# Moving the product with V from the end of a block to the middle of its score products, in a two-pass attention kernel

## What is computed

```python
x = x + layernorm(attn(layernorm(x)))        # 16 heads of 8 features, 512 x 512 scores per head
x = x + layernorm(ffn(layernorm(x)))         # 128 x 128 products, one sigmoid gate, relu squared
# attn: q = x@Wq+bq ; k = (x@Wk+bk)@Wl+bl ; v = (x@Wv+bv)@Wl+bl
#       softmax(q k^T / sqrt(8)) v, then @ Wo + bo
```

## Time and profile before

| | |
|---|---|
| median of 3 runs | 268.84 us (265.88 to 268.85) |
| the profiled execution | 269.19 us, of which the span of the core 267.3 us |
| share of the span busy | PE 94%, DVE 76%, ACT 67%, PEld and POOL 37% each |
| chain of work that ended last | PE 78%, DVE 13%, ACT 3% |

### The profile page before, as it was taken

How to read it: one execution, slowest core, us unless ns; L and a number is a source line. 1 busy time by engine, 2 the same in 40 slices (tenths; PEclk the granted TensorE clock), 3 DMA queues, 4 the chain that set the end, 5 groups by cost and what they waited for, 6 DMA issues and landing times.

```text
span 267.3 us, 4825 instructions
## 1 busy us (share of the span) xinstructions
PE 250.5 (94%) x1383; PEld 97.6 (37%) x1383; DVE 203.7 (76%) x366; ACT 179.6 (67%) x352; POOL 98.1 (37%) x227
## 2 busy tenths in 40 slices
PE   8996979999999999999999999999999999898981
PEld 4552532232323253234332432343324323332560
DVE  2699688888787888988689889886898998614525
ACT  2573658887787776787677767767677677695132
POOL 6847463010101015551215355512153545214623
PEclk9997799999999999999999999999999999999799
DMA  5346727222030303030304120303031000000101
GB/s 157 99 137 174 213 56 207 60 56 80 13 92 3 88 4 88 2 92 3 88 4 88 41 88 2 88 2 88 2 88 42 2 2 1 4 0 1 39 2 40
DMA packets 13814, 15.65 MB, mean 59 GB/s; under 512 B 3153, under 2 KB 11346, under 8 KB 13794
## 3 DMA queue, kind: packets, MB, share of 16 engines
q1 hardware_dynamic: 13218, 15.15, 20.9%
q10 hardware_dynamic: 576, 0.26, 0.3%
HBM read 11.01 MB, written 4.19 MB: 57 GB/s over the span
## 4 chain that ended last, share of the span: by engine, by line
PE 78%; DVE 13%; ACT 3%; issue 3%; POOL 2%; POOLq 0%; DVEq 0%; ACTq 0%
PE psO L1294 22%; PE psB L1282 20%; PE psA L1263 18%; DVE mx L952 6%; PE psM L1177 3%; PE psM L1183 3%; DVE xh L898 2%; PE psA L1163 2%; ACT pT L805 1%; PE psO L1201 1%; PE psM L1210 1%; PE psM L1243 1%; POOL rs_x L512 1%; PE psA L1422 1%; PE psA L1466 1%
## 5 line engine op out<-in xcount | busy, mean ns | idle before, releaser
L952 DVE TENSOR_REDUCE mx<-psA 128x2 f32<-128x1024 f32 x128 | 151.4, 1219 | 32.0 <-PE psA L1263 31.4
L805 ACT ACTIVATE pT<-psB 128x512 f32<-128x512 f32 x244 | 132.6, 597 | 37.2 <-PE psB L1282 36.6
L1282 PE MATMUL psB<-QS,KS 75*128 75x512 bf16 x244 | 92.7, 384 | 0.8 <-ACT pT L805 0.3
L1263 PE MATMUL psA<-KS,QS 72*128 72x512 bf16 x256 | 89.3, 386 | 2.8 <-DVE mx L952 1.9
L1294 PE MATMUL psO<-pT,Vg 128*32 128x512 f32 x512 | 68.2, 604 | 0.3
L1282 PEld LDWEIGHTS psB<-QS,KS 75*128 75x128 bf16 x244 | 23.2, 97 | 79.1 <-ACT pT L805 59.1
L1263 PEld LDWEIGHTS psA<-KS,QS 72*128 72x128 bf16 x256 | 25.1, 99 | 24.7 <-DVE mx L952 6.1
L505 POOL TENSOR_TENSOR mm<-mx,one 128x16 bf16<-128x16 f32 x16 | 3.4, 215 | 39.3 <-DVE mx L952 39.3
L1294 PEld LDWEIGHTS psO<-pT,Vg 128*32 128x32 f32 x512 | 10.2, 108 | 21.0 <-issue 16.1
L544 POOL TENSOR_TENSOR Vg<-v_st,one 128x128 f32<-128x128 f32 x16 | 6.2, 398 | 27.5 <-PE psO L1294 27.5
L1163 PE MATMUL psA<-warm 128*128 128x512 bf16 x40 | 12.1, 464 | 1.2 <-DVE warm L916 1.2
(11 more groups left out here) (179 smaller groups left out, 265.7 us busy)
## 6 DMA issues: line engine op xcount, KB each, us to landing
KS<-k_scr SPq DMA_DIRECT2D x45, 96.0 KB
QS<-q_scr SPq DMA_DIRECT2D x15, 288.0 KB
k_scr<-kp SPq DMA_DIRECT2D x12, 128.0 KB, 2.3
q_scr<-qp SPq DMA_DIRECT2D x12, 128.0 KB, 2.3
x_all<-in_L_attn_x_dram SPq DMA_DIRECT2D x4, 256.0 KB, 3.2
out_dram<-out_sb SPq DMA_DIRECT2D x3, 256.0 KB, 2.3
KS<-k_scr SPq DMA_DIRECT2D x6, 48.0 KB
QS<-q_scr SPq DMA_DIRECT2D x2, 144.0 KB
```

Of the source, the lines that this page charges most:

```text
L805: nc.scalar.activation(pT[:, n % 2, i, :], score_bank(n, i, last), ACT.Exp, scale=SCALE).then_inc(e_rdy, 1)
L952: nc.vector.tensor_reduce(out=mx[:, g % 2, c:c + 2], in_=psA[:, u, :, :], axis=AX.X, op=ALU.max).then_inc(a_max, 1)
L1263: score = nc.tensor.matmul(psA[:, u, j, :], QS[g][0:ROWS, h, P * t:P * (t + 1)], KS[g][0:ROWS, h, :], start=True, stop=True)
L1282: nc.tensor.matmul(score_bank(n, i, last), KS[g][0:KEXP, i, P * t:P * (t + 1)], QS[g][0:KEXP, i, :], start=True, stop=True).then_inc(b_rdy, 1)
```

## The change

PV of the block behind is no longer issued at the end of a block, between the job places 3 and 4, but in its middle, after m01 and ahead of job place 0:

```diff
                     for_maxima(0, 0)
                     for_exponentials(1)
                     for_maxima(0, 1)
+                    if n or not first:
+                        times_v_before(b, n, first)
                     jobs(n, 0)
                     for_maxima(1, 0)
                     jobs(n, 1)
...
                         pe.wait_ge(q_tak, 2 * NB)
                     jobs(n, 3)
-                    if n or not first:
-                        times_v_before(b, n, first)
                     jobs(n, 4)
```

## The result

| | before | after |
|---|---|---|
| median | 268.85 us (265.88 to 269.41, 4 runs) | 298.26 us (293.76 to 299.06, 4 runs) |
| the profiled execution | 269.19 us, span 267.3, mean granted clock 0.979 | 297.68 us, span 295.9, clock 0.972 |

The ratio is 1.102, with a 95% interval of 1.084 to 1.121: the change costs about 10%. It compares fast executions alone and leaves out the two after the change (298.84 and 299.06 us) that were slower at a mean clock of 0.968; 293.76 and 297.68 are left. The forecast was 295 us, in a range of 289 to 301.

The account below looks back on a forecast made before the run. It took PE, 94% busy, as the bound, with the two psB banks' reuse only just covered. Terms 25.1 - 5.75 + 0.9 + 1.5 - 0.8 + 2.8 + 2.0 = +25.8 on 269.2 gave 295 us, range 289 to 301.

Parts of the forecast that it names:

- The plain block: Blocks without jobs: PE stands 0.50 us before e0; period 3.40 against 2.96 us, 57 x 0.44 = +25.1 us.
- e0: First of a block's four score products on PE; forecast to start 1.16 us after the third of the block before.
- the ring: Two psB banks: a score product may follow the one two before it only after its exponential, 1.16 us; batch 0, 1.10.
- Jobs behind e3: Jobs after a block's last score product fill PE's gap before e0, saving up to 0.55 us each: -5.75 us.
- Rival 2: Jobs at a block's end do not cover the gap, their ACT copies preceding the next exponentials: +5.75, 301 us; 10%.
- r behind m3: Job r waits for ACT's copy of job m3, starting 0.65 us behind it instead of 0.15: 0.45 x 2 = +0.9.
- Block 1: Batches 1, 2, 3: PV(0) waits for the psO copy, 1.70 us after the second score product, before 0.54; net +2.8.
- The tail: End of the last batch, four banks: PV waits for exponentials and the psO copy, partly offset at job m3; +2.0 us.
- The clock: Whole kernel: granted clock stays 1.00 as long as waits stay well under 1 us; no term in the sum.
- rival 4: PE's short stands drop the clock to 0.50, +2.1 us a block; one block in ten gives +13, 308 us; 5%.
- 1 (special places free): Block 1, the tail and r's wait cost nothing: 289 us; 12%.
- 3 (not slower): PE's order costs nothing and the present 0.11 us shortfall goes: 265 us, needing 0.66 or less for 1.16; 2%.

Follow-up runs that it names:

- mended: Changed kernel with the psO copy in block 1 and job m3 one place earlier, PV at the block's end again from block 10 of the last batch: 290.06 us.
- mended2: Changed kernel with the psO copy in block 1 one place earlier, PV at the block's end again from block 11 of the last batch: 289.62 us.
- m_end: Changed kernel with only the block's last two products for maxima moved, each behind the score product it preceded, PV still in the middle: 288.06 us, one run.
- swap_wait: Kernel before the change with ACT's two waits ahead of an exponential swapped in all batches, the PV wait only at a block's first: 269.47 us, ratio 1.001.
- loop_swap: Kernel before the change with ACT's two waits swapped only in the loop (batches 1 and 2): 267.61 us against 269.31, ratio 0.992.
- mirror: Changed kernel with PV still in the middle and the four products for maxima reordered around it: 292.2 us median.
- mirror_all: mirror's order plus earlier psO copy and job m3, PV at the block's end in the last batch's tail, ACT's waits swapped, DVE jobs moved: 280.0 us, one run.

## Why the forecast was right, point by point

**The plain block.** Right in its mechanism and in each distance but one. e1 came 0.49 behind e0, PV did not wait in a plain block, PE stood between e3 and e0, and the stand did not come back elsewhere. The turned order, one product more under e2 to e0 and the half-width exponentials each shortened the block, to 2.89, 3.10 and 3.05 from 3.32. The size was off in the loop: e2 to e0 was taken as 1.16, the ring of before, and it was 1.07. I had put the 1.16 down to the product and the bank; a part of it, 0.08, was the extra step of ACT's first exponential, and the change moved the wait to an exponential without it. In batch 0 the 1.10 read from the rows was no measure of the ring, since PE's own five products take that long; behind the change it was 1.07 there too, which alters little. So a loop block cost 0.36, not 0.44; in batches 0 and 3 it cost the 0.44. The term is 32 x 0.36 + 25 x 0.44 = 22.5, not 25.1. It was a sum over 57 blocks, so an error of 0.08 in one row became 2.6 us.

**Jobs behind e3.** They covered the gap as worked out, with one exception: in batch 0 e0 of block 11 waited for the exponential of e2, which stands on ACT behind the copy of what m3 wrote. Timeline of PE, m3 and e0:

```profile
76.40 0.22 PE L1223 MATMUL psM<-ident_b,mm 128*128 128x128 bf16 x1
77.46 0.39 PE L1282 MATMUL psB<-QS,KS 75*128 75x512 bf16 x1 [0.84 <-ACT pT L805]
```

That block took 3.96 instead of 3.32, +0.64, a term the sum lacked. In the mended kernel it was 3.75. Rival 2 described this very effect, but for all jobs; it held for one.

**r behind m3.** 134.10 to 134.75, the 0.65 that was forecast, with PE's wait put down to ACT's copy mmT.

**Block 1.** Timelines of PE (e1, PV(0)) and of ACT (the copy of psO):

```profile
98.38 0.39 PE L1282 MATMUL psB<-QS,KS 75*128 75x512 bf16 x1
...
99.98 1.06 PE L1294 MATMUL psO<-pT,Vg 128*32 128x512 f32 x8 [0.99 <-issue]
...
99.30 0.58 ACT L781 COPY o_sb<-psO 128x512 f32<-128x512 f32 x1
```

PV came 1.60 behind e1, forecast 1.70, and the block was 1.07 longer than a plain one. The sum had 2.8 for three of them, net of the 0.21 or so that each cost before; 3 x 1.07 less that is 2.6. Mending the place took the 1.07 away, so its cause is shown.

**The tail.** Forecast +2.0, measured +2.75: from e2 of block 9 to the end of the last PV, 19.4 us before and 22.1 after. Up to e0 of block 11 it got 0.6 shorter, where the forecast had -0.5 at m3 (PE still waited 0.41 there). The waits behind it have the expected places and about their sizes: 1.05 for the copy of psO at PV(12), forecast 1.1; 0.53 for the exponential at PV(13), forecast 0.65; and 0.96 at PV(15), part of the forecast's 1.64 from e2:

```profile
263.95 1.07 PE L1294 MATMUL psO<-pT,Vg 128*32 128x512 f32 x8 [1.05 <-ACT o_sb L781]
...
267.50 1.06 PE L1294 MATMUL psO<-pT,Vg 128*32 128x512 f32 x8 [0.53 <-ACT pT L805]
...
273.10 1.07 PE L1294 MATMUL psO<-pT,Vg 128*32 128x512 f32 x8 [0.96 <-ACT pT L805]
```

What went wrong is the comparison behind e2 of block 14. From there to the end it took 5.13 us before and 5.68 after, as forecast (5.1 and 5.7). But the stretch before holds three PVs (13, 14 and 15) and the stretch after two: PV(13) now lies ahead of that e2, and its 1.0 us was added nowhere. With it the term would have been +3.0.

**The clock.** The sum had nothing for it, and rival 4 had a block in ten at half speed, +13, at 5%. The profiled execution lost 2.74 us in one fall. Of the four executions one has a mean clock of 0.990 and took 293.76 us; the others have 0.968 to 0.972, and only one was traced. The forecast's condition, waits well under 1 us, was broken by its own block 1, where PE stands 0.99: the fall came right behind that stand in batch 2, and not behind the same stand of batch 1 and of batch 3. With that stand mended (`mended2`) the clock did not fall between 48 and 280 us, and its four runs lie within 0.6%. That does not show the stand as the cause, since `m_end` keeps all three stands of 0.99 us and its trace has no fall behind any of them. Nor is every fall the change's: `mended2` has one from 42.0 to 45.4 us, and six of the eleven traces have one that begins between 39 and 42 us, in the first blocks, among them `swap_wait` and `loop_swap`, which have PV at the block's end. The stands of the plain blocks, 0.41 us and some forty times, came with no fall in `mended2` from 48 to 246 us: the granted clock of that window is 1.00. The section of the Trainium skill that the prediction cited ("TensorE: Matmul & The Clock Gate", "A second HAM failure mode: psum-queue depth-cycling") would have put all of these blocks at risk; the trace of `mended2` shows it for none of those between 48 and 246 us.

**The sum.** The forecast from profile to profile was +25.8 and 28.5 was measured. Too much by 2.6 in the plain blocks; too little by 0.64 for m3 in batch 0, 0.75 in the tail and 2.74 for the clock, which makes +27.3. Of the remaining 1.2 us about 0.5 is the ring of the loop again, as an estimate: with 1.07 instead of 1.16 a long job behind e3 can save 0.46 us and not 0.55, and there are six of them (y, r and kf in two batches). The rest is spread over the blocks with jobs and was not followed further. The 295 was near partly by luck, because errors of both signs met.

**The rivals.** 1 (special places free) fell: block 1 and r's wait cost about what their chains said, and the tail more. 2 (jobs don't cover) held for one job in one batch. 3 (not slower) would have needed a ring of 0.66; even with half-width exponentials it was 0.87 and the order still cost 0.21 a block. 4 happened in small.

## What to carry to other kernels

When a consumer empties few banks, measure the distance between two products into the same bank and list what lies in it, for each pair of uses: the sum of a block's work does not show which distance is short. An instruction that is moved to a place where cover is plentiful takes away no work but uncovers the place it left, once in every iteration. And when a queue starts to wait at another instruction than before, the latency to use is that instruction's, with its own waits, not the one measured at the old place.

## What the runs showed of the hardware that was not expected

Two waits on one ACT instruction are not free, and their order matters. In the loop, where a wait compares with a register, waiting last for the semaphore that really comes last made the exponential start 0.43 instead of 0.51 us after the product, and the loop 0.6 us shorter. With constants the same swap cost 0.06 instead. The traces show where the sign comes from: ahead of the exponential ACT's sequencer has a step of its own that carries one of the two waits, and what costs is that step behind the product. Before, in the loop, it is the arithmetic for `pv_done` and it waits for the product; in `swap_wait`, in batch 0, it is a bare wait, and again it is the one for the product. The first exponential starts 0.08 us behind that step in the one and 0.06 in the other. Line L804 there, first before, then in `swap_wait`:

```profile
L804 ACTq ALU_OP  x1: 35/35/35, 111.0 to 111.0; - x1
...
L804 ACTq EVENT_SEMAPHORE  x1: 17/17/17, 64.7 to 64.7; - x1
```

In the two other cases (before in batch 0, `swap_wait` in the loop) the step waits for `pv_done` and is done before the product is. So the order in the program does not say which wait the step carries; the trace does.

The granted clock fell to 0.50 behind single stands of PE of 0.99 us in the changed kernel, 1.26 in `mirror`, and at stands of 1.59 and 1.58 at m3 in `mended` and `mirror_all`, and stayed there for 6.8 us (3.4 in `mirror_all`). But most stands of that size had no such effect: two more of 0.99 us in the changed kernel, three of 0.99 in `m_end`, 1.22 and 1.26 in `mirror`, and 1.15 before. And in `mirror` it also fell at 41 us, in the first blocks, where PE had stood only 0.61 and 0.25 us. A stand of about 1 us does not by itself bring the fall; what decides it stays open.
